# The set-up of a two-layer attention kernel cut into five parts, with most of it moved into the first steps of the trunk

## The reference

```python
x = x + _L0_xattn_ref(ctx_1024, _layernorm(x), ctx_1024, Wq, Wk, Wv, Wo)   # causal, 16 heads of 64
x = x + _L0_ffn_ref(_layernorm(x), w_gate, w_up, w_down)                   # fp4_quant_dequant of inputs and weights
x = x + _L1_xattn_ref(_layernorm(x), ctx_1024, ...)                        # text and image keys
x = x + _L1_ffn_ref(_layernorm(x), ...)                                    # 8 experts, top 2
```

## Time and profile before

| | |
|---|---|
| runs | 695.01, 696.79, 702.23 us |
| median | 696.79 us |
| the profiled execution | 698.52 us |
| its span, first to last instruction | 696.8 us |
| around the span | 1.7 us |
| mean granted TensorE clock | 0.976 |
| PE, DVE, ACT, POOL busy | 90%, 76%, 63%, 43% of the span |

### The profile page before, as it was taken

How to read it: one execution, slowest core, us unless ns; L and a number is a source line. 1 busy time by engine, 2 the same in 40 slices (tenths; PEclk the granted TensorE clock), 3 DMA queues, 4 the chain that set the end, 5 groups by cost and what they waited for, 6 DMA issues and landing times.

```text
span 696.8 us, 16585 instructions
## 1 busy us (share of the span) xinstructions
PE 628.6 (90%) x5849; PEld 573.1 (82%) x5849; DVE 531.8 (76%) x1454; ACT 438.9 (63%) x1121; POOL 297.9 (43%) x428
## 2 busy tenths in 40 slices
PE   3779999989899989999999999999999998979980
PEld 2678888878788888999999989988888977979980
DVE  7896677788898888988899898797666574665655
ACT  3668787878777777555565655555755545656660
POOL 3133444435434343353444442335327475465550
PEclk9989999999999999999999999999999999999995
DMA  9700000000000000206666131000000001212215
GB/s 232 224 1 1 1 3 1 1 3 1 1 2 1 2 16 1 99 25 127 129 112 123 29 104 50 1 1 2 1 1 32 24 25 47 58 55 63 71 52 184
DMA packets 49389, 33.27 MB, mean 48 GB/s; under 512 B 9414, under 2 KB 45868, under 8 KB 49308
## 3 DMA queue, kind: packets, MB, share of 16 engines
q1 hardware_dynamic: 47036, 27.55, 16.5%
q0 software_dynamic: 2272, 4.67, 2.0%
HBM read 17.57 MB, written 14.63 MB: 46 GB/s over the span
## 4 chain that ended last, share of the span: by engine, by line
PE 50%; DVE 16%; issue 14%; ACT 8%; POOL 8%; DMA 2%; SPq 1%; POOLq 0%; DVEq 0%; ACTq 0%
PE ps_j L402 6%; PE ps_s L569 5%; PE ph L1466 5%; ACT scores L782 5%; PE py L1477 5%; DVE scores L1041 5%; PE ps_h L641 4%; PE ps_t L605 4%; PE ps_h L620 4%; PE ps_j L364 4%; POOL probs L1303 3%; POOL xs_scratch L1395 3%; PE ps_j L366 3%; PE ps_j L365 3%; DVE neg_max L1048 3%
## 5 line engine op out<-in xcount | busy, mean ns | idle before, releaser
L1303 POOL TENSOR_TENSOR probs<-scores,rsums 128x308 f32<-128x308 f32 (+1 forms) x192 | 152.8, 811 | 227.7 <-DVE rsums L1061 227.3
L1056 DVE TENSOR_REDUCE sums<-scores 128x4 f32<-128x308 f32 (+1 forms) x192 | 90.7, 500 | 40.7 <-ACT scores L782 34.6
L605 PE MATMUL ps_t<-ident,probs 128*128 128x128 f32 x512 | 79.2, 277 | 19.9 <-ACT probsT L796 16.9
L782 ACT ACTIVATE scores<-scores,neg_max 128x128 f32<-128x128 f32 x256 | 81.6, 393 | 18.1 <-DVE neg_max L1048 17.6
L669 ACT ACTIVATE QT<-ps_j 128x512 f32<-128x512 f32 x64 | 38.3, 598 | 82.1 <-PE ps_j L366 82.1
L605 PEld LDWEIGHTS ps_t<-ident,probs 128*128 128x128 f32 x512 | 58.4, 142 | 26.1 <-issue 21.1
L796 ACT ACTIVATE probsT<-ps_t 128x512 f32<-128x512 f32 x128 | 75.4, 589 | 6.3 <-PE ps_t L605 6.3
L569 PE MATMUL ps_s<-KT,QT 64*128 64x128 f32 x1024 | 75.6, 288 | 0.8 <-ACT KT L675 0.8
L620 PE MATMUL ps_h<-probsT,V 128*64 128x128 f32 x1024 | 70.9, 281 | 0.8 <-DVE x_sb L827 0.8
L569 PEld LDWEIGHTS ps_s<-KT,QT 64*128 64x128 f32 x1024 | 63.2, 190 | 8.9 <-issue 2.4
L641 PE MATMUL ps_h<-Wo,headsT 128*128 128x128 f32 x512 | 69.1, 278 | 0.0
(11 more groups left out here) (239 smaller groups left out, 1616.3 us busy)
## 6 DMA issues: line engine op xcount, KB each, us to landing
xs_scratch<-xs SPq DMA_DIRECT2D x8, 1032.0 KB, 8.3
xt<-xs_scratch SPq DMA_DIRECT2D x39, 64.5 KB
w1b<-in_L_ffn_w_dram SPq DMA_DIRECT2D x1, 2048.0 KB, 9.8
big_raw<-in_L_ffn_w_dram SPq DMA_DIRECT2D x8, 256.0 KB, 4.7
ysum<-y_scratch SPq DMA_DIRECT2D x4, 512.0 KB, 5.4
x_sb<-in_x_dram SPq DMA_DIRECT2D x4, 256.0 KB, 4.0
ctx_sb<-in_ctx_dram SPq DMA_DIRECT2D x4, 256.0 KB, 4.8
Wo<-in_L_xattn_Wo_dram SPq DMA_DIRECT2D x2, 512.0 KB, 6.6
```

Source lines behind the costliest of these rows:

```text
L605: ins = nc.tensor.transpose(ps_pT[:, j * S:(j + 1) * S], probs[s % 2][:, j, :], ident[:, :])
L782: ins = nc.scalar.activation(scores[s % 4][:, j, :], scores[s % 4][:, j, :], ACT.Exp, bias=neg_max[:, s % 4, 0, j:j + 1])
L1056: ins = nc.vector.tensor_reduce(sums[:, p4, i, :], scores[p4][:, :, k0:k1], AX_X, ALU.add)
L1303: ins = nc.gpsimd.tensor_tensor(probs[(s - 1) % 2][:, :, k0:k1], scores[r][:, :, k0:k1], rsums[:, r, i, :].rearrange("p (h a) -> p h a", a ...
```

## The change

Set-up is cut into five parts of batches instead of four quarters, `PARTS`: 2, 2, 4, 4 and 4 batches. Only part 0 stands before the trunk. Parts 1 to 4 begin in steps 0, 3, 17 and 20 (`PART_AT`), each spread over three steps: in the first, statistics (DVE part 1), the power on POOL at the end of its step, and normalisation (DVE part 3); in the second, transposes on PE and high parts on ACT; in the third, low parts (DVE part 0). The transposes use the two banks `pf` of the feed-forward layer. The first-layer weights are loaded and split in halves of 512 columns; ACT makes all six high halves before the trunk's first copy, and DVE makes five low halves before the trunk and the sixth in step 0. The weight quantisation and its transposes move by one group: parts 0 to 2 to step 7, parts 3 to 20 to steps 8 to 13. The loads are reordered. The waits for set-up become waits at the projections and at POOL's staging. The set-up's buffers move into the space of the second layer's split weights. A second load of the exponential table goes.

```diff
+PARTS = [(0, PAIR), (PAIR, PAIR), (QUAD, QUAD), (2 * QUAD, QUAD), (3 * QUAD, QUAD)]
+        PART_AT = {1: 0, 2: 3, 3: 17, 4: 20}
+        def part_transpose(pe, p):
+            b0, nb = PARTS[p]
+            pe.wait_ge(s_ctx[p], 16)
+            wait_pos(pe, NS["lo"], p)
+            wait_pos(pe, s_ctx_lo, p)
...
+            for b in range(nb):
+                ins = nc.tensor.transpose(pf[1][:, b * S:(b + 1) * S], ctx_sb[:, b0 + b, :], ident[:, :])
+            ins.then_inc(s_ctxp, 1)
+            pe.wait_ge(NS["xn"], p + 1)
+            for b in range(nb):
+                ins = nc.tensor.transpose(pf[0][:, b * S:(b + 1) * S], xn_sb[p % 2][:, b, :], ident[:, :])
+            ins.then_inc(NS["xnT"], 1)
+        def setup_scalar(act):
+            w0_high(act, 0)
+            part_high(act, 0)
+            for j in range(1, 6):
+                w0_high(act, j)
+        def setup_vector(dve):
+            statistics(dve, 0)
+            normalise(dve, 0)
+            w0_low(dve, 0)
+            part_low(dve, 0)
+            for j in range(1, 5):
+                w0_low(dve, j)
@@ project_q, project_k, project_v in trunk_tensor
+                if lay == 0:
+                    pe.wait_ge(NS["lo"], part_of(g) + 1)
+                if lay == 0 and g == 0:
+                    pe.wait_ge(s_split0_lo, split_of(0, hb))
@@ step in trunk_tensor
-                if first:
+                if G == 1:
                     weights_transpose(pe, s)
+                p, t = part_at(n)
+                if t == 1:
+                    part_transpose(pe, p)
-            pe.wait_ge(NS["lo"], QUADS)
-            pe.wait_ge(s_ctx_lo, QUADS)
-            pe.wait_ge(s_split0_lo, 3)
@@ step in trunk_scalar, behind the exponentials
+                p, t = part_at(n)
+                if t == 1:
+                    part_high(act, p)
...
-            nc.scalar.preload_act_table(ACT.Exp)
@@ step in trunk_vector
                 def part(i):
-                    if first and i > 0 and 2 + 3 * s + i < 21:
+                    if n == STEPS - 1 and i > 0:
+                        quantise_weights(i - 1)
+                    if G == 1 and i > 0 and 2 + 3 * s + i < 21:
                         quantise_weights(2 + 3 * s + i)
-                    if first and i == 0:
+                    if G == 1 and i == 0:
                         weights_low(dve, s)
+                    p, t = part_at(n)
+                    if t == 0 and i == 1:
+                        statistics(dve, p)
+                    if t == 0 and i == 3:
+                        normalise(dve, p)
+                    if t == 2 and i == 0:
+                        part_low(dve, p)
+                    if n == 0 and i == 2:
+                        w0_low(dve, 5)
@@ step in trunk_gpsimd, behind the probabilities and the raw weights' split
+                p, t = part_at(n)
+                if t == 0:
+                    rstd_part(pool, p)
@@ block.sync
+            load_x(0)
+            load_w0(0)
+            load_ctx(0)
+            load_w0(1)
+            load_w0(2)
+            load_w0(3)
+            load_w0(4)
+            load_x(1)
+            load_ctx(1)
+            load_w0(5)
+            load_x(2)
+            load_ctx(2)
             sp.wait_ge(s_fz, 1)
...
             sp.dma_start(dw_raw[:, :], w_down).then_inc(s_fw[2], 16)
+            for p in (3, 4):
+                load_x(p)
+                load_ctx(p)
             sp.dma_start(Wo[0][:, :, :], L0_Wo.rearrange("(t p) n -> p t n", p=P)).then_inc(s_wo0, 16)
             for name, w in (("Wq", L1_Wq), ("Wk", L1_Wk), ("Wv", L1_Wv), ("Wk_ip", L1_Wk_ip), ("Wv_ip", L1_Wv_ip)):
                 sp.dma_start(big_raw[:, L1_W[name]:L1_W[name] + INNER], w).then_inc(s_big1, 16)
```

More of the change, by code:

```diff
@@ L204, in build_program @@
         rsums = sbuf("rsums", [P, 4, 2, HB], F32, mem)
-        mem.close()
-        mem = ExitStack()
-        pn = psum_banks([f"pn{i}" for i in range(8)], mem)
         mem.close()
@@ L366, in three_pass, with quad, span, part_of @@
             return nc.tensor.matmul(psum, hi[:, w_cols], act_hi, start=False, stop=stop)
+        NS = {k: sem(f"norm0_{k}") for k in ("stats", "rstd", "xn", "xnT", "hi", "lo")}
+        norm_chain = sem("norm0_chain")
+        def quad(q):
+            return slice(q * QUAD, (q + 1) * QUAD)
+        def span(p):
+            return slice(PARTS[p][0], PARTS[p][0] + PARTS[p][1])
+        def part_of(g):
+            return next(p for p, (b0, nb) in enumerate(PARTS) if b0 <= g * PAIR < b0 + nb)
+        PART_AT = {1: 0, 2: 3, 3: 17, 4: 20}
@@ new lines, in setup_tensor, with statistics @@
+        def setup_tensor(pe):
+            pe.wait_ge(s_const, 2)
+            part_transpose(pe, 0)
+        def setup_scalar(act):
[3 more added lines that the diff above has]
+                w0_high(act, j)
+        def statistics(dve, p):
+            b0, nb = PARTS[p]
+            dve.wait_ge(s_x[p], 16)
+            for b in range(b0, b0 + nb):
+                ins = nc.vector.bn_stats(stats[:, b, :], x_sb[:, b, :])
+            ins.then_inc(norm_chain, 1)
+            dve.wait_ge(norm_chain, 2 * p + 1)
+            for b in range(b0, b0 + nb):
+                ins = nc.vector.bn_aggr(mean_var[:, b, :], stats[:, b, :])
+            ins.then_inc(norm_chain, 1)
+            dve.wait_ge(norm_chain, 2 * p + 2)
+            nc.vector.tensor_scalar(rstd[:, span(p)], mean_var[:, span(p), 1], EPS, None,
+                                    ALU.add).then_inc(NS["stats"], 1)
@@ new lines, in weights_high @@
+        def weights_high(act, s):
+            if s in (2, 4):
+                i = s // 2 - 1
+                act.wait_ge(SS["wT_ready"], i + 1)
+                nc.scalar.activation(guT_hi[:, i, :], pf[i][:, 0:FF], ACT.Copy).then_inc(SS["w_hi"], 1)
+            if s == 7:
+                act.wait_ge(SS["wT_ready"], 3)
+                for t, (r0, rn) in enumerate(FT):
+                    ins = nc.scalar.activation(dnT[0:rn, t, :], pf[0][0:rn, t * P:(t + 1) * P], ACT.Copy)
+                ins.then_inc(SS["w_hi"], 1)
```

246 lines of the change are left out of this document (112 added, 134 removed).

## The result

The median went from 697.83 us (695.01 to 702.39) to 703.52 us (700.84 to 704.53), 20 executions each. The ratio is 1.0064, with a 95% interval of 1.0050 to 1.0078, that is +4.5 us (3.5 to 5.4). The medians themselves lie 5.7 apart; where the two differ I go by the ratio, which has an interval. The prediction was 701 us and +4.1. The profiled execution took 701.96 us, with a span of 700.2.

What follows compares the result with a forecast made beforehand. PE is busy 90%, but the first 114 us were taken as bound by a closed DVE-ACT loop with 2.46 us DVE idle per pair. -8.4 + 4.4 + 8.1 = +4.1 on the median 696.79 gave 701 us, range 691 to 708.

Steps and rivals of the forecast that it cites:

- -8.4 + 4.4 + 8.1: Sum over the start of group 1, group 1's length and group 2's length: +4.1 us.
- Part 1, the start: Set-up: trunk starts when the last weight half lands, at 12.1; first mask at 16.0 against 26.26, 10.3 us earlier.
- Part 2, group 0: Group 0: POOL stands 6 us for big_raw, delaying step 3's normalisation; mask of step 6 at 42.5, group 1 8.4 us earlier.
- the bound 11.1: Group 0: if big_raw did not hold POOL, normalisation comes 2.7 us earlier and group 1 begins 11.1 us earlier.
- parts 0 to 2 of the quantisation in steps 6 and 7: End of group 0: 1.75 us of work, within the pair's 2.46 us of DVE idle time, so free.
- Part 3, group 1: Group 1 takes the 18 parts of quantisation that group 0 had: plus 4.4 us, about 31.7 us long.
- Part 4, group 2: Group 2: set-up parts 3 and 4 meet the feed-forward layer; 3.8 + 1.0 + 3.3, plus 8.1 us.
- the 0.8 us for a tensor_scalar held by the power: Step 20: the tensor_scalar behind q_max is held until POOL's power is done, 0.8 us of that pair's plus 3.3.
- rival B: Group 2, steps 18 and 21: PE's clock falls after stalls, 2.4 us each, together +4.8, 705.7 us; chance 0.18.
- A: Group 2: new pieces fill idle time, plus 1.6 us instead of 8.1, sum -2.4, 694.4 us; chance 0.22.
- C: Start: last half lands late; big_raw's stall hides about 3.8 us of slip, start at 26 gives 709 us; chance 0.1.
- the upper bound of group 1: Group 1: plus 4.9 us over three plain pairs, with nothing taken off for the lowered clock.

Runs made afterwards that it cites:

- run 2: Changed kernel with part 4's context transposes made seven times instead of once, keeping PE busy in step 20; ratio to the kernel before 1.0051.
- Run 8: As run 7, but ACT makes only high halves 1 and 2 ahead of its first Q and K copies; 685.33 us, ratio to the kernel before 0.9849.
- run 1: Changed kernel with POOL's split of raw weights moved to s = 5 and 6 in groups 0 and 2; ratio to the kernel before 1.0024.
- run 6: Changed kernel once more, unchanged; 703.16 us in its one execution.
- Run 3: Changed kernel with all 21 parts of the weight quantisation in steps 0 to 6 of group 0 again; ratio to the kernel before 1.0088.
- Run 5: As Run 3, with parts 3 and 4 in steps 10 to 16, normalisation two steps after statistics, weights' transposes in steps 9 and 11; ratio to before 0.9991.
- run 4: Changed kernel with the last half of the value weights loaded behind part 2's x and context; ratio to the kernel before 1.0073.
- run 10: As Run 8, with the down weights' quantisation given the other tile of scales, so nothing is overwritten; 684.03 us, ratio to the kernel before 0.9858.
- run 7: Changed kernel with Run 5's parts 3 and 4, run 1's split, part 2's normalisation a step later, quantisation spread to step 24; 689.96 us, ratio 0.9905.

## Why the prediction was right, and where its steps were not

**The sum.** -8.4 + 4.4 + 8.1 was +4.1. At the mask of step 24 the trace has -7.92 + 4.38 + 9.00 = +5.46; timed, it is +4.5 (3.5 to 5.4). The second trace of the kernel after has +6.92. Without the fall of the clock (run 2) the mask comes at +3.25. So the three parts were read rightly in the main, and that +4.1 lies so near +4.5 is in part luck: the start of group 1 was 0.5 us too early in the sum, group 2 without the fall was 1.4 us too dear (8.1 for 6.7), and the fall of the clock, which adds 2.2, was left to a rival.

**Part 1, the start.** Predicted 16.0, measured 15.84. Run 8 shows what set it: with two instead of five high halves ahead of the Q copy the mask comes at 12.93. The landing of the last half was the right place to look; the timeline of ACT has its high part at 12.02, released by the transfer, where I had the landing at 12.1:

```profile
12.02 0.63 ACT L436 ACTIVATE l_hi<-w_raw 128x512 fp32r<-128x512 f32 x1 [1.47 <-DMA w_raw<-in_L_xattn_Wv_dram]
```

**Part 2, group 0.** POOL stands at `big_raw` for 4.62 us instead of 6, its copy at 27.52 instead of 28.6 (5.59 and 28.88 in the second trace); DVE's normalisation came at 32.74, predicted 32.5, and the mask of step 6 at 42.17, predicted 42.5. But the chain that I wrote is not the one that ran. I forgot an instruction: the low part of the raw weights, 1.54 us at 30.20, stands ahead of the power in step 3. Above I gave its place as s = 5; in the first layer it is s = 3 (the second layer has the copy at 5 and the low part at 6). And the landing, 1.1 earlier than I took it, would have made up for most of that. I also gave the stand for `big_raw` 2.7 us as its price (the bound 11.1); run 1 shows 0.8, since DVE's statistics hold the inverse sums nearly as long. With the later landing of run 6 the same working gives some 1.8, an estimate: DVE's inverse sums are at 28.38 there, so without the stand the probabilities would end near 29.8 and not at 31.55. Nor did the K copy set step 4, as I had it (36.7, by PE's low clock): it ended at 34.81, and the exponentials began at 36.34, behind the row maxima. Two errors cancelled, and the right end time was no proof of the chain.

A term that failed in the total: I called the parts 0 to 2 of the quantisation in steps 6 and 7 free. Their pair took 7.66 us, and a plain one 6.83. Timeline of DVE in it:

```profile
46.85 0.99 DVE L1030 TENSOR_SCALAR q_scale<-q_scale 128x24 f32<-128x24 f32 x1
```

And of POOL:

```profile
46.77 1.04 POOL L1492 TENSOR_TENSOR probs<-scores,rsums 128x512 f32<-128x512 f32 x1 [2.71 <-DVE rsums L1237]
```

A tensor_scalar of 24 columns takes 0.99 us, because it is issued 0.08 behind POOL's probabilities and ends with them (47.81); free it takes 0.17 to 0.18. I had the mechanism from the earlier trace rows and priced these parts without it. The hold explains the 0.8 us by its size; no run takes it out. So group 1 began 7.92 earlier, not 8.4.

**Part 3, group 1.** Predicted plus 4.4 (31.7 us), measured 31.69. Run 3, which has the quantisation in group 0, leaves 27.99: so 3.7 us of the 4.4 are the quantisation, and 0.7 the weights' transposes with their high and low parts, which I had not priced apart.

**Part 4, group 2.** Predicted 10.6, 8.4, 11.1 and 6.8 for its pairs; measured 10.19, 8.38, 12.28 and 7.06. The first is the mechanism that I costed, to be seen in the timeline of DVE:

```profile
85.40 0.86 DVE L452 BATCH_NORM_STATS2 stats<-x_sb 128x6 f32<-128x128 f32 x4
89.75 1.12 DVE L467 TENSOR_SCALAR xn_sb<-x_sb,mean_var,rstd 128x128 f32<-128x128 f32 x4 [2.80 <-POOL rstd L495]
```

And of POOL:

```profile
87.03 1.04 POOL L1492 TENSOR_TENSOR probs<-scores,rsums 128x512 f32<-128x512 f32 x1 [3.63 <-DVE rsums L1237]
88.02 0.72 POOL L1511 CAST l_hi<-big_raw 128x640 fp32r<-128x640 f32 x1
88.70 1.02 POOL L495 TENSOR_TENSOR rstd<-rstd,minus_half 128x4 f32<-128x4 f32 x1
```

Probabilities, copy, power, in this order, and DVE waits 2.80 us for them (predicted 3.1, though its terms add up to 3.2): plus 3.4 us instead of 3.8. Run 5, which puts a step between statistics and normalisation, has this wait gone. The high parts of step 18 cost 0.97 (predicted 1.0), and the low parts of step 23 were free, as predicted (6.82 us in run 2).

The pair of step 20 was mis-sized in two terms that go against each other. First, the 0.8 us for a tensor_scalar held by the power do not exist; timeline of POOL in the kernel after:

```profile
104.44 1.01 POOL L495 TENSOR_TENSOR rstd<-rstd,minus_half 128x4 f32<-128x4 f32 x1 [2.36 <-DVE rstd L459]
```

And of DVE:

```profile
104.72 0.17 DVE L1027 TENSOR_SCALAR q_scale<-q_scale 128x16 f32<-128x16 f32 x1
104.92 0.17 DVE L1030 TENSOR_SCALAR q_scale<-q_scale 128x16 f32<-128x16 f32 x1
105.48 1.11 DVE L467 TENSOR_SCALAR xn_sb<-x_sb,mean_var,rstd 128x128 f32<-128x128 f32 x4
```

Both run at full speed while POOL takes its power. So the pair should cost 2.5 more than before, and runs 2, 3 and 4, where the scores behind the idle of step 21 ran at full clock, have 10.22, 10.22 and 10.23: plus 2.4 over 7.86. Second, rival B came true in one of its two places: the fall of the clock adds 2.06 us (12.28 less 10.22). I had given B 0.18, since the only long idle in the trace of before was 4.29 us; 3.02 was enough. B's price of 2.4 was near, its condition ("if a stall comes near 4.3 us") was wrong. This fall is the term that the sum put at nothing; with it group 2 is +9.0, without it +6.7, predicted +8.1.

**Rivals A and C.** A, that the pieces would fill idle time, is false for the places that the change chose, and true for others: run 5 gets parts 3 and 4 for 2.4 us where 7.6 us of DVE work are new, and run 10 has all of the work in three groups of 88.5 us together, where before took 87.7, and 1.2 more behind them. C's cover is real but was taken too large: 3.8 us by the prediction, 0.88 of a slip of 1.76 us in run 4, for the same reason that the stand costs so little. The start was not late. (By C's own rule a start at 26 gives 707 us, not 709, and B with the upper bound of group 1 is 706, not 708; nothing in the forecast rests on these.)

**What stays open.** Whether the clock falls in step 21 in each execution of the kernel after. In both profiles it did. The two have +5.46 and +6.92 at the mask of step 24, both above the timed +4.5 (3.5 to 5.4), and run 2 without the fall has +3.25; that the timed runs are a mixture is only argued, and so is the share that the landing of `big_raw` has in it. The kernel before has one trace, so what its own mask varies by is not known.

## What to carry to other kernels

In a closed loop between engines the place of a new piece counts more than its length: steps 2 to 7 took 26.14 us with statistics and normalisation of part 2 in one step (run 1), and 21.24 with a step between them and the other pieces spread (run 7). Moved to another group as well, parts 3 and 4 cost 2.4 us instead of 9.0, of which the low clock was 2.2. Put a step between the request to a slow engine and its use, and read what that engine has ahead in its order, every instruction of it, a wait for a transfer first of all. When PE gets idle time of 2 to 3 us from such a wait, count the low clock behind it too. And compare two kernels at marks inside the trace; the ends of two profiles here differed by 3.4 us for the same work. Even such a mark moved by 1.46 us between two traces of one kernel, because a transfer landed later.

## What the runs showed of the hardware

**The power doesn't hold DVE.** A tensor_scalar beside POOL's power took 0.17 us, beside POOL's probabilities 0.99. The Trainium skill, "SBUF — State Buffer", section "Who interferes with whom", says that the pair of ports that DVE and POOL share goes to whoever issues first, for the whole instruction, while the other one is blocked; it makes no exception among the POOL instructions that read SBUF. By it the tensor_scalar at 104.72, if it is one that needs the pair, as the one at 46.85 seems to, would have waited to 105.45. It did not. So the trace doesn't agree for the power of 128x4 elements, and agrees for the probabilities of 128x512, and for the raw weights' low part (in run 3 DVE's sum of `fw_raw` and `q_c`, 128x384, took 1.77 us beside it, and one of that shape 0.55 with POOL idle). It is not the shape on DVE's side: in run 3 the tensor_scalar of 128x24 took 0.19 us at 19.99, beside a power of 128x2 that ran from 19.96 to 20.66, and DVE's subtraction with two SBUF inputs at 20.44, inside that power too, took 0.63, no longer than elsewhere (0.69 at 19.10 in the kernel after). The other way round there is some hold: a power of 128x2 takes 0.70 us in run 3 and 1.07 in the kernel after (at 19.27), where such a subtraction began 0.17 ahead of it; and one of 128x4 takes 1.32 in run 3 instead of 1.01, beside the sum that ran to 36.76. Whether DVE is spared because of the operation or because of POOL's small size, no run tells apart.

**An idle time of the same length lowers the clock or not.** In step 19 PE stood 2.61 us in the kernel after and 2.60 in run 4; in step 21 2.16 in run 1 and 2.17 in run 4. The timeline of PE in the kernel after, step 19:

```profile
96.56 0.63 PE L782 MATMUL ps_t<-ident,probs 128*128 128x128 f32 x4 [2.61 <-ACT probsT L973]
```

In run 4, steps 19 and 21:

```profile
97.38 1.08 PE L782 MATMUL ps_t<-ident,probs 128*128 128x128 f32 x4 [2.60 <-ACT probsT L973]
...
107.99 0.66 PE L424 MATMUL pf<-ident,xn_sb 128*128 128x128 f32 x4 [2.17 <-DVE xn_sb L467]
```

And in run 1, step 21:

```profile
106.54 1.11 PE L424 MATMUL pf<-ident,xn_sb 128*128 128x128 f32 x4 [2.16 <-DVE xn_sb L467]
```

Of the two rows of each step one runs at the high level and one at the low, behind the same idle. What differs there between the kernels is little but when it happens. The Trainium skill, "TensorE: Matmul & The Clock Gate", section "What's actually happening", says that the chip's watch over activity runs freely and doesn't start with the kernel, so that the moment of a change varies; by that rule equal idle times may come out either way, and these rows agree. A fall in step 19 costs 0.2 to 0.7 us (8.56, 8.88 and 9.12 us for the pair in runs 3, 4 and 1, 8.38 in after). Runs 1, 3 and 4, which had it (granted clocks 0.81, 0.86 and 0.81), had a shorter idle in step 21 (2.16, 1.69 and 2.17 us instead of 3.02). In runs 3 and 4 the transposes behind it ran at full clock, in run 1 at the low one, and its pair took 11.28 us. I read the shorter idle as PE being late from step 19 on, which no run isolates. Which of the two steps is hit decides up to 2 us, though group 2 began only 0.83 us later in run 4 than after (82.35 for 81.52).

**The clock can fall with PE busy.** In both profiles of the kernel after, the router's matmuls of 8 columns near 510 us were followed by scores at low clock; before they were not. Timeline of PE, after:

```profile
509.87 1.85 PE L661 MATMUL pf<-rw_sb,hidT 128*128 128x8 f32 x16
511.64 1.90 PE L743 MATMUL ps_s<-KT,QT 64*128 64x128 f32 x16
```

And before:

```profile
504.45 1.85 PE L487 MATMUL pf<-rw_sb,hidT 128*128 128x8 f32 x16
506.23 1.16 PE L569 MATMUL ps_s<-KT,QT 64*128 64x128 f32 x16
```

The same 16 small matmuls, the same 1.85 us; then 1.90 for 1.16. In the kernel after PE was busy for 6.59 of the 6.64 us ahead of these scores, at a granted clock of 1.00; behind them, from 511.64 to 513.47, the clock is 0.56. By the transposes that follow (at 516.38, before at 509.42) the shift has grown by 1.5 us, and it shows in no busy share. In the ten traces of the other kernels the same scores took 1.16 us, and other such groups of 16 small matmuls (at 532.12 in the kernel after) were not followed by the low clock, so what makes it fall here is not shown.
